# Second attention's context tiles normalised at the head of the first expert stage; the keys' stage turns them at once and stores the second batch's part first

## The reference

```python
x = x + L0_xattn(layernorm(x), ctx)              # cross attention, 16 heads of 16
x = x + L0_ffn(layernorm(x))                     # 16 routed experts, 4 a token, and one shared
x = x + L1_xattn(ctx, mask, layernorm(x))        # keys: [LN(ctx); LN(layernorm(x))], queries from x
x = x + L1_ffn(layernorm(x))                     # 8 routed experts, 2 a token, and one shared

def L1_xattn(features, masks, latents):
    f   = _layernorm(features, gm, bm)           # (v - mean) * rsqrt(var + 1e-5) * gamma + beta
    lat = _layernorm(latents, gl, bl)
    q   = lat @ Wq
    kv  = concatenate([f, lat], axis=1)          # 512 context keys, then 512 of x
    k, v = kv @ Wk, kv @ Wv
    ...
```

## Time and profile before

| | |
|---|---|
| three timed runs | 3389.04, 3395.5, 3395.71 us, median 3395.5 |
| the profiled execution, its own time | 3391.4 us |
| its span, first to last instruction | 3389.7 us |
| mean granted TensorE clock | 0.956 of full |
| busy share | PE 93%, PEld 68%, DVE 65%, ACT 40%, POOL 49% |

### The profile page before, as it was taken

The page is one execution under the profiler, slowest core; times in us unless marked ns, Lnnn a source line. Parts: engine busy times, 40 slices in busy tenths (PEclk is TensorE's granted clock), DMA queues, the critical chain, the costliest instruction groups (busy, mean ns, idle before and its releaser), DMA issues. The chain is left out here.

```text
span 3389.7 us, 58855 instructions
## 1 busy us (share of the span) xinstructions
PE 3139.7 (93%) x18285; PEld 2303.0 (68%) x18286; DVE 2195.8 (65%) x5104; ACT 1343.8 (40%) x2058; POOL 1659.5 (49%) x1001
## 2 busy tenths in 40 slices
PE   5885999999879999999999999999999977889978
PEld 4655888888756666666666666666666656679966
DVE  5657555555657777777777777777776663245545
ACT  2332333333334444444444444444444432234422
POOL 5002333333236666666666666666666655770047
PEclk7995999999989999999999999999999977989999
DMA  4000000001111111212111112121111032342253
GB/s 114 1 0 5 17 12 14 9 14 59 75 57 63 63 63 38 78 47 81 38 63 62 64 37 83 42 84 35 66 63 50 11 110 83 129 157 71 73 179 104
DMA packets 118348, 204.62 MB, mean 60 GB/s; under 512 B 13792, under 2 KB 85544, under 8 KB 112432
## 3 DMA queue, kind: packets, MB, share of 16 engines
q1 hardware_dynamic: 105200, 173.30, 15.1%
q0 software_dynamic: 12992, 29.72, 3.0%
HBM read 141.28 MB, written 61.64 MB: 60 GB/s over the span
## 5 line engine op out<-in xcount | busy, mean ns | idle before, releaser
L2279 POOL TENSOR_TENSOR d_acc<-d_acc,d_pr 128x1024 f32<-128x1024 f32 x384 | 938.7, 2444 | 90.4 <-ACT d_pr L2133 59.6
L2133 ACT ACTIVATE d_pr<-d_p 128x1024 f32<-128x1024 f32 x512 | 487.9, 1027 | 242.1 <-PE d_p L2060 241.0
L1993 PE MATMUL d_pO<-d_pr,d_V 128*64 128x512 f32 x2048 | 473.0, 599 | 0.0
L2279 POOL TENSOR_TENSOR d_acc<-d_pr 128x1024 f32<-128x1024 f32 x64 | 153.5, 2398 | 624.4 <-ACT d_pr L2133 624.4
L2189 DVE TENSOR_REDUCE d_nm<-d_p 128x2 f32<-128x1024 f32 x256 | 304.5, 1222 | 94.9 <-PE d_p L2036 94.9
L940 POOL TENSOR_TENSOR e_hs<-e_hf,e_hs 128x512 fp32r<-128x512 f32 x136 | 175.9, 1294 | 364.9 <-ACT e_hs L915 364.9
L2184 DVE CUSTOM_DVE_ANT_0 d_biased<-d_p,d_masked 128x512 f32<-128x512 f32 x512 | 330.6, 688 | 27.9 <-issue 25.4
L1993 PEld LDWEIGHTS d_pO<-d_pr,d_V 128*64 128x64 f32 x2048 | 135.4, 136 | 261.5 <-issue 233.0
L970 DVE SCALAR_TENSOR_TENSOR res<-e_pY,m_Wt,res 128x256 f32<-128x256 f32 x544 | 225.8, 477 | 45.8 <-PE e_pY L876 45.0
L2200 DVE RECIPROCAL d_rb<-d_rb 128x128 f32<-128x128 f32 x256 | 224.6, 920 | 7.5 <-ACT d_rb L2126 7.5
L961 DVE TENSOR_TENSOR e_hf<-e_sl,e_pU 128x512 f32<-128x512 f32 x136 | 93.7, 689 | 207.7 <-ACT e_sl L912 207.7
(11 more groups left out here) (333 smaller groups left out, 5856.7 us busy)
## 6 DMA issues: line engine op xcount, KB each, us to landing
d_W<-w_split SPq DMA_DIRECT2D x30, 1536.0 KB, 6.9
d_masked<-mask_bias SPq DMA_DIRECT2D x64, 256.0 KB
kv_split<-d_parts SPq DMA_DIRECT2D x56, 256.0 KB, 5.2
d_kv<-kv_split SPq DMA_DIRECT2D x7, 2048.0 KB, 11.1
x_slots<-m_zeros SPq DMA_DIRECT2D x1, 9088.0 KB, 26.8
b_x<-x_slots SPq DMA_DIRECT2D x71, 128.0 KB, 2.0
y_slots<-b_y SPq DMA_DIRECT2D x71, 128.0 KB, 1.7
xh_split<-m_XH SPq DMA_DIRECT2D x8, 1024.0 KB, 4.4
```

What stands on the lines that cost most here:

```text
L1993: last = pe.matmul(pO[own[h], :], V[vb][:, s, par * P + h * HD1:par * P + (h + 1) * HD1], pr[:, s % PT, h, :], start=(s == 0), stop=(s == ...
L2133: act.activation(pr[:, n % PT, :, :], slot(st, what, n)[:, :, :], ACT.Exp).then_inc(exp_done, 1)
L2279: pool.tensor_tensor(acc[:, q, :, :], a, pr[:, s % PT, :, :], ALU.add).then_inc(acc_done, 1)
```

## The change

Four edits in one.

1. **Context tiles early.** The eight loads into `cin` leave `Ahead.sync` and stand in the m0 routes' block, after the gate and the first expert's weights. `Ahead.normalise`, called on DVE ahead of the first `mult` of e0, takes mean and variance of the eight tiles, finds the reciprocal root by a bit guess and three Newton rounds on a 128x8 tile (no ACT), and writes the normalised tiles back in place.
2. **Keys' block.** `JOBS` is now ((1, 0), (0, 0), (0, 1)): PE turns the two context jobs from `cin` at once, DVE normalises only the four tiles of `res`, and the store of `later` waits for the first low part alone.
3. **First expert's weights early.** `FirstExpert` owns the raw buffers. Its loads stand in the routes' block of both layers. For ea (`split=True`) the high parts are made on ACT behind the eight batches, ahead of `route1`'s own ACT operations, and the low parts on POOL behind its loop. For e0 (`split=False`) the split stays at the head of the experts' block. eb is as before.
4. Single weight buffers where there is one expert.

```diff
@@ moe_routes
                 sp.dma_start(gate[:, :, :], io[f"{tag}_gate"]).then_inc(gate_in, 16)
+                first.load(sp)
+                if beside:
+                    beside.load_inputs(sp)
                 r["sync"](sp)
...
                         ins.then_inc(lo_done, 1)
+                first.low(pool)
...
                 for_batches(act, emit)
+                first.high(act)
                 r["scalar"](act)
@@ moe_experts, scalar and gpsimd
-                split(0, 0)
+                if loads or not first.split:
+                    split(0, 0)
@@ moe_experts, vector
+                beside.normalise(dve)
                 mult(0, 0, 0)
@@ class Ahead
+    def normalise(self, dve):
+        n, c = 2 * TPB, Counted(self.cstep)
+        tile = lambda i: self.cin[:, i // TPB, i % TPB, :]
+        step = lambda ins: dve.wait_ge(c.sem, c.done(ins))
...
+        for i in range(n):
+            m = c.done(dve.bn_stats(self.st[:, i, :], tile(i)))
+        dve.wait_ge(c.sem, m)
+        for i in range(n):
+            m = c.done(dve.bn_aggr(self.mv[:, i, :], self.st[:, i, :]))
+        dve.wait_ge(c.sem, m)
+        step(dve.tensor_scalar(self.v[:, :], self.mv[:, :, 1], 1.0, EPS, ALU.mult, ALU.add))
+        step(dve.tensor_scalar(self.z[0][:, :].bitcast(mybir.dt.int32), self.v[:, :].bitcast(mybir.dt.int32), -0.5,
+                               GUESS, ALU.mult, ALU.add))
+        for r, (add, by) in enumerate(((-3.0, -0.5), (-3.0, -0.5), (-3.0, -0.5))):
+            z, z_next = self.z[r % 2], self.z[1 - r % 2]
+            step(dve.tensor_tensor(self.t[:, :], z[:, :], z[:, :], ALU.mult))
+            step(dve.tensor_tensor(self.t[:, :], self.t[:, :], self.v[:, :], ALU.mult))
+            step(dve.tensor_scalar(self.t[:, :], self.t[:, :], add, by, ALU.add, ALU.mult))
+            step(dve.tensor_tensor(z_next[:, :], z[:, :], self.t[:, :], ALU.mult))
+        for i in range(n):
+            c.done(dve.tensor_scalar(tile(i), tile(i), self.mv[:, i, 0:1], self.z[1][:, i:i + 1], ALU.subtract,
+                                     ALU.mult))
@@ Ahead.sync
-        self.load(sp, 0, 0)
-        self.load(sp, 1, 1)
@@ layer1_keys_in
-JOBS = ((0, 0), (0, 1), (1, 0))
+JOBS = ((1, 0), (0, 0), (0, 1))
...
-                sp.wait_ge(y_lo, NJ)
+                sp.wait_ge(y_lo, 1)
                 sp.dma_start(kv_d[1][:, :, :, 0:S], later[:, :, :, :].bitcast(F32)).then_inc(kv_out, 16)
...
-                root(0)
-                root(1)
                 act.wait_ge(gb_in, 16)
-                take(0)
-                root(2)
-                take(1)
-                take(2)
+                act.wait_ge(var, 1)
+                act.activation(ve[:, :], ve[:, :], ACT.Sqrt).then_inc(sd, 1)
+                for j in range(NJ):
+                    take(j)
...
-                spread(0)
-                spread(1)
-                normalise(0)
-                spread(2)
-                normalise(1)
-                normalise(2)
...
-                    pe.wait_ge(xhat, TPB * (j + 1))
+                    if m:
+                        pe.wait_ge(xhat, TPB)
```

More of the change, by code:

```diff
@@ L547, in moe_routes @@
+def moe_routes(nc, io, res, ident, XH, Wt, tag, E, route, first, rows=None, beside=None):
     with ExitStack() as ctx:
@@ L984, in _ @@
                 for_units(dve, emit)
+GUESS = float(0x5F3759DF)
 class Ahead(Nothing):
@@ L1044, in layer0_ffn @@
         XH = sb("m0_XH", [P, 2, DC, B * S], F32R)
-        moe_routes(nc, io, res, ident, XH, Wt, "m0", E0, route0)
-        moe_experts(nc, io, res, ident, XH, Wt, "e0", N0, I0, beside=ahead)
+        first = FirstExpert(sb, sem, io, "e0", "e0", 0, I0, False)
+        moe_routes(nc, io, res, ident, XH, Wt, "m0", E0, route0, first, beside=ahead)
+        moe_experts(nc, io, res, ident, XH, Wt, "e0", N0, I0, beside=ahead, first=first)
 class Plan:
@@ L1661, in _ @@
-                spread(2)
-                normalise(1)
-                normalise(2)
+                for t in range(TPB):
+                    dve.bn_stats(st[:, t, :], res[:, t, :]).then_inc(stats, 1)
+                dve.wait_ge(stats, TPB)
+                for t in range(TPB):
+                    dve.bn_aggr(mv[:, t, :], st[:, t, :]).then_inc(moments, 1)
+                dve.wait_ge(moments, TPB)
+                dve.tensor_scalar(ve[:, :], mv[:, :, 1], 1.0 + EPS, EPS * EPS, ALU.mult, ALU.add).then_inc(var, 1)
@@ L1664, in _ @@
+                dve.wait_ge(sd, 1)
+                dve.reciprocal(rs[:, :], ve[:, :]).then_inc(rstd, 1)
+                dve.wait_ge(rstd, 1)
+                for t in range(TPB):
+                    dve.tensor_scalar(xh[:, t, :], res[:, t, :], mv[:, t, 0:1], rs[:, t:t + 1], ALU.subtract,
+                                      ALU.mult).then_inc(xhat, 1)
                 for j in range(NJ):
```

150 lines of the change are left out of this document (87 added, 63 removed).

## The result

The changed kernel takes 3369.98 us (median of 5 runs, 3368.73 to 3376.11) against 3389.26 us for the kernel before on the same chip (5 runs, 3389.04 to 3395.71): ratio 0.9941, interval [0.9928, 0.9954]. Run once more in the experiments it took 3368.57 us, ratio 0.9931 [0.9918, 0.9943] against 15 runs of before there (median 3392.31). So it is 19 to 24 us faster; 17.0 us were forecast, to 3376.5 us, and the time lies inside the range, towards its fast end. The profiled execution has a span of 3367.1 us, before it was 3389.7 us.

What follows compares the result with a forecast made beforehand. PE's standstills in the keys' block and the heads of e0 and ea were taken as what the change can shorten: 11.2 + 0.8 + 5.0 = 17.0 us, from 3393.5 to 3376.5 us, range 3368.5 to 3383 us.

Steps and rivals of the forecast that it cites:

- Keys' block, 11.2 us forecast: Keys' block: ACT's three jobs, then DVE's last low part, set its end, with the store landing just before; 11.2 us gained.
- ACT's square root ... stays at 920.88 us: Keys' block: statistics of `res` take the same DVE time as those before, so the root starts unchanged, ending at 921.08 us.
- e0's head, 0.8 us forecast: Head of e0's experts: weights come 1.5 us earlier, but DVE's added work ends 0.7 us after the product could start.
- whatever the head of that block gains or loses is passed on in full: e0's experts: PE is busy for the whole 530 us of the bulk at full clock, which the change cannot shorten.
- ea, 5.0 us forecast: Head of ea's experts: 7.8 us gained, less 2.7 us lost in layer 1's routes, taken as 5.0 us for the clock.
- The collision: Layer 1's routes: POOL's subtractions and three DVE operations with two SBUF inputs take turns, so ea starts 2.7 us later.
- The rule cited there: Layer 1's routes: a two-SBUF-input DVE instruction contends with a GpSimd SBUF read; the later is blocked fully until the first ends.
- if some block that is not touched, the pairs above all, took a different time for starting elsewhere: Blocks outside the change: a sign that the prediction was wrong; no gain or loss was forecast for them.
- POOL harmless: Layer 1's routes: POOL does not hold up DVE, so ea gains 7.8 us, 19.8 us in all, 3373.7 us; chance 0.15.
- The store 5 us late at the end of the keys' block: Keys' block: the store of `c_later` takes 10 us, landing 5.1 us after DVE's end; 11.9 us gained, 3381.6 us; chance 0.12.
- DVE's head so slow that the kernel loses: e0's head: each of 14 dependent DVE steps costs 2.02 us, first product 25.2 us late, 3401.7 us; chance 0.03.
- The gate late: Routes: the gate tile arrives behind ten more transfers; 3 us late would cost 1 us in a stage; no chance given.

Runs made afterwards that it cites:

- root_before_gains: Changed kernel with ACT's wait for the gains' load moved behind the square root in the keys' block; 3369.13 us, ratio 0.9934.
- again: The changed kernel, unaltered, run and profiled once more; 3368.57 us, ratio to before 0.9931.
- norm_in_routes: Changed kernel with the context tiles' normalisation moved from e0's head into DVE's pause in layer 0's routes; 3369.31 us, ratio 0.9933.
- best: Changed kernel, normalisation and e0's first-expert rounding and split moved into layer 0's routes, plus the edits of low_after_choice and root_before_gains; 3365.93 us, ratio 0.9925.
- low_after_choice: Changed kernel with POOL's three subtractions for ea waiting until DVE has made the second `m_hot`; 3368.33 us, ratio 0.9930.

## Why the prediction came out as it did

**Keys' block, 11.2 us forecast, 10.3 measured.** The chain was the one described (ACT, then DVE's last low part, the store off the path); two sizes in it were off, in opposite directions. "ACT's square root ... stays at 920.88 us" was wrong: its table load now waits for the variances, 1.34 us, shown by root_before_gains. Without that the block gains 11.7 us, 0.5 more than forecast, since a job costs ACT 2.42 us in place of 2.50 and the turn to the next block, counted from DVE's end, 1.2 in place of 1.45 us. By the prediction's own sign, the next block's start after 12.4 to 13 us, the block was just outside with 13.30 us.

**e0's head, 0.8 us forecast, 1.3 to 2.0 measured at the first product, 0.6 in the block.** DVE is the last link, as forecast: the product waits 0.5 us for it in "again" (nothing in after, where SiLU was late), and its work is 0.6 us shorter than reckoned. Over four traces of before and its variants the first product comes 10.71 to 11.18 us after the start, over six with the normalisation once at the head and the weights split there 9.21 to 9.42 us. The whole of e0, to the keys' block, was 583.13 to 583.58 us in the four and 582.22 to 583.47 us in the six. The step "whatever the head of that block gains or loses is passed on in full" held, but two costs that the prediction didn't have stand at the block's end. From the first product to the keys' block the four take 572.40 to 572.42 us. The turn to the keys' block (DVE's idle time ahead of its first row there) grew from 1.54 to 1.95 us in all ten traces with the change. And the last down projection, twelve matmuls, takes 1.70 us in before and up to 2.92 us in the others; here are before, at a granted clock of 1.00 of full speed over these matmuls, and after, at 0.51.

```profile
913.02 1.70 PE L876 MATMUL e_pY<-e_Wd,e_hs 128*128 128x256 f32 x12 [1.98 <-POOL e_hs L940]
```

```profile
910.78 2.92 PE L934 MATMUL e_pY<-e_Wd,e_hs 128*128 128x256 f32 x12 [1.97 <-POOL e_hs L1000]
```

In "again" they took 1.90 us at 0.85, in norm_in_routes 1.75 us, in best 1.69 us. Together the two account for all of the entry of +1.63 us in the first table: 0.41 us for the turn and 1.22 us for the matmuls. The same sum gives this stretch within 0.03 us in the eight other traces with one normalisation. Why the clock falls there in most traces with the change, and why the turn is longer, stays open.

**ea, 5.0 us forecast, 6.8 measured (5.6 in "again").** The 7.8 us at the head are there to the hundredth. The collision was real (low_after_choice) and 1.8 us instead of 2.7: I had DVE's and POOL's pieces take turns in full. In the first execution 0.7 us of it came back by luck, through the higher clock of the four matmuls behind it, so that only 1.08 us show in the block. In fact the third DVE operation was done at 2802.97 us, only 0.4 us after POOL, and POOL's pieces took 5.5 us with two DVE operations among them, where 5.1 + 1.0 were reckoned. The rule cited there gave the three operations, and all three were held up. That the later one is blocked, and in full, the rows don't settle. In the row of 2.02 us that stood for it, the DVE operation had started 0.67 us ahead of POOL's subtraction and was the one held up. And here the first and the third operation ended 0.3 and 0.4 us after POOL's piece, less than the 0.42 and 0.60 us that they take alone. The 0.1 us for the clock is what varies: ea's first product differs by up to 1.1 us between executions.

**Outside the change, 0 forecast, 3.2 to 3.9 us measured.** That is what the prediction's last sentence named as the way to be wrong: "if some block that is not touched, the pairs above all, took a different time for starting elsewhere". It did, and the runs with memsets point not to its start in time but to the place of its code. It is most of what is left between the 17.0 us forecast and the 19 to 24 us measured. The changed blocks alone, 0.8 + 11.2 + 5.0 by forecast, gave -0.3 + 10.3 + 6.8 = 16.8 us in the profiled execution (e0 counted to its end) and 0.9 + 10.3 + 5.6 = 16.8 us in "again". That this is so near 17.0 is in part luck: the table load's 1.3 us and e0's end cost what shorter jobs, a milder collision and the clock gave back. The base of 3393.5 us was high too, by 4.2 us against the median timed with the result (3389.26 us) and by 1 to 3 us against the later ones (3390.97 to 3392.31 us).

**The rivals.** POOL harmless: out, the three rows show it. The store 5 us late at the end of the keys' block: out, though it ends within 0.2 us of DVE. DVE's head so slow that the kernel loses: out, its 14 steps cost 0.20 us each. The gate late: out, layer 0's routes took 77.66 us in both.

## What to carry to other kernels

- When a wait is moved or added on ACT ahead of an activation that needs another table, look where the table load stands: it may take the wait with it, and 1.3 us come onto the path.
- Price a block's head from several executions before saying who ends last there; the granted clock moved ea's first product by up to 1.1 us, as much as some edits did.
- A change can alter the time of a loop that it doesn't touch by moving its code. If a stage far from the edit changes by the same few microseconds in every variant, count the packets of the instruction queue (`q14` here) and put some idle instructions into the program of before.

## What of the hardware was not expected

- **Loads of code in a loop.** DVE stood still for 1.1 to 1.8 us once in eight steps, with one packet of the instruction queue during the stand-still or just ahead of it. Two more instructions ahead in the program moved all six stand-stills by one recorded instruction, ten removed them, for 2.6 to 3.7 us in the block. The Trainium skill, page "Advanced Engine Details and Errata", section "ISA Cache", says that an engine has only two cache lines, each of 256 instructions. That a stand-still hangs on the place of the code fits it, as does the loop: some 400 recorded DVE instructions lie from one stand-still to the next, and 656 if the waits and branches in the trace are counted, more than two such lines would hold. The size of a line is shown by no run here (a packet is 0.95 MB / 116 = 8.2 KB), nor why ten instructions suffice.
- **A tensor_scalar beside POOL.** Eight normalisations, one tensor and two columns of scalars in SBUF each, took 4.46 and 5.82 us in place of 2.67 us beside two and four of POOL's subtractions. The Trainium skill, page "SBUF — State Buffer", section "Who interferes with whom", counts tensor_scalar among the operations that may take the port shared with GpSimd; the rows agree. I had looked for the cost only in operations with two tensors.
- **A table load that waits** with the instruction it serves: with two waits ahead of that instruction the load began at 920.31 us, 2.1 us into the block and behind the variances; with one, at 917.51 us, the block's start.
